# A two-layer graph network whose second neighbour list is gathered in groups of one chunk in place of two

## The reference

```python
x_l = x @ W_l.T + b_l                                    # layer 0
agg = segment_sum(x_l[src], dst)                         # sum over the edges into dst
x = layernorm(x + agg / max(deg, 1)[:, None] + x @ W_r.T)
msg = h[dst] @ W_neigh.T + b_neigh                       # layer 1, h = x
neigh = segment_sum(msg, src)                            # sum over the edges out of src
out = relu(h @ W_self.T + b_self + neigh / max(deg, 1)[:, None])
x = layernorm(x + layernorm(h + out) * gamma + beta)
```

## Time and profile before

| | |
|---|---|
| median of 3 runs | 4260.94 us (4256.3 to 4261.07) |
| span of the profiled execution | 4265.6 us |
| layer 0, placing woven in | 518 to 1850 us |
| layer 0, rest of its chunks | 1850 to 1990 us |
| layer 0, projection | 1990 to 2386 us |
| layer 1, gathering of 928 chunks | 2391 to 3806 us |
| layer 1, projection | 3806 to 4266 us |
| busy in the span: PE, DVE, ACT, POOL | 65%, 61%, 19%, 44% |

### The profile page before, as it was taken

One profiled execution on the slowest core, in us unless ns is written; L12 is line 12 of the kernel. 1 busy time (PEld: TensorE's weight loads), 2 busy tenths in 40 slices (PEclk: granted clock), 3 DMA queues, 4 the chain that ended last, 5 costly groups with the idle time before them and its releaser, 6 DMA issues.

```text
span 4265.6 us, 57125 instructions
## 1 busy us (share of the span) xinstructions
PE 2781.9 (65%) x11308; PEld 1195.8 (28%) x11308; DVE 2610.8 (61%) x6523; ACT 815.1 (19%) x2156; POOL 1897.4 (44%) x2073
## 2 busy tenths in 40 slices
PE   1000188888888888866999655555555555568887
PEld 0000033333333333322455211112111111124443
DVE  3878877777777777754555444444444444448887
ACT  0300044444444444410222000000000000002222
POOL 0600166666666666664000366666666666630000
PEclk9555599999999999977999765665566665669999
DMA  3300066656656666664333566666666666671111
GB/s 140 121 0 0 25 166 166 167 162 165 166 164 164 166 167 166 165 203 136 98 103 103 156 175 178 173 175 173 175 176 176 175 174 170 168 115 59 59 59 49
DMA packets 201222, 586.38 MB, mean 137 GB/s; under 512 B 34672, under 2 KB 35502, under 8 KB 201196
## 3 DMA queue, kind: packets, MB, share of 16 engines
q0 software_dynamic: 148480, 488.56, 42.3%
q1 hardware_dynamic: 52716, 97.53, 7.3%
HBM read 534.51 MB, written 51.44 MB: 137 GB/s over the span
## 4 chain that ended last, share of the span: by engine, by line
PE 39%; DVE 19%; issue 16%; DMA 10%; DVEq 6%; another core or an unknown queue 4%; ACT 2%; SPq 2%; POOL 2%; POOLq 0%; ACTq 0%
PE ps L703 37%; DMA rows<-table,idx_ring 8%; DVE acc L577 4%; DVEq L571 3%; DVE flat L496 2%; DVE onehot L564 2%; POOL rows L359 2%; DVE flat L497 1%; DVE flat L498 1%; DVE where L592 1%; PE ps L805 1%; DVE st L651 1%; PE ps L808 1%; DVE spot L590 1%
## 5 line engine op out<-in xcount | busy, mean ns | idle before, releaser
L359 POOL DMA_INDIRECT rows<-table,idx_ring x1856 | 1794.6, 967 | 1438.0 <-issue 453.5
L703 PE MATMUL ps<-rows,onehot 128*128 128x512 f16 (+1 forms) x5568 | 1378.6, 384 | 782.5 <-DVE acc L577 614.7
L577 DVE TENSOR_TENSOR acc<-acc,ps 128x513 f32 x928 | 638.7, 688 | 850.8 <-remote 328.4
L703 PE MATMUL ps<-where,put 128*128 128x464 f16 x3328 | 801.1, 363 | 380.3 <-ACT put L852 297.8
L703 PEld LDWEIGHTS ps<-rows,onehot 128*128 128x128 bf16 x5568 | 537.3, 113 | 1645.9 <-DVE acc L577 749.2
L564 DVE TENSOR_SCALAR onehot<-iota_node,loc_ring,rows 128x128 bf16<-128x128 f16 x1856 | 583.4, 322 | 281.2 <-DMA rows<-table,idx_ring 250.1
L851 ACT ACTIVATE put<-spot,flat 128x128 f16<-128x128 f16 x832 | 334.1, 402 | 1099.4 <-DVE spot L590 754.3
L703 PEld LDWEIGHTS ps<-where,put 128*128 128x128 f16 x3328 | 267.4, 97 | 696.5 <-issue 371.3
L592 DVE TENSOR_SCALAR where<-iota_chunk,hi_ring 128x928 f16<-128x928 f16 x832 | 380.4, 457 | 0.0
L865 ACT ACTIVATE flat<-acc,rdeg 128x512 f32 (+1 forms) x98 | 69.4, 710 | 1577.5 <-DVE rdeg L640 1574.0
L703 PE MATMUL ps<-w_a,flat 128*128 128x512 f32 x784 | 355.1, 596 | 0.1
(11 more groups left out here) (131 smaller groups left out, 1368.0 us busy)
## 6 DMA issues: line engine op xcount, KB each, us to landing
rows<-table,idx_ring POOLq DMA_INDIRECT x1856
table<-rows SPq DMA_DIRECT2D x98, 257.0 KB, 3.7
h_scratch<-rows SPq DMA_DIRECT2D x49, 256.0 KB, 2.0
rows<-h_scratch SPq DMA_DIRECT2D x49, 256.0 KB, 2.7
acc<-in_x SPq DMA_DIRECT2D x4, 3072.0 KB, 23.5
rows<-in_x SPq DMA_DIRECT2D x48, 256.0 KB, 3.3
out<-rows SPq DMA_DIRECT2D x48, 256.0 KB, 2.0
w_a<-in_w_l_t SPq DMA_DIRECT2D x1, 1024.0 KB
```

What stands on the lines that cost most here:

```text
L359: nc.gpsimd.indirect_dma_start(out=rows[:, k % GB, :], out_offset=None, in_=tables[layer][:, :], in_offset=bass.IndirectOffsetOnAxis(ap=id ...
L577: V.tensor_tensor(tile_acc, tile_acc, part, ALU.add).then_inc(s_acc, 1)
L703: return nc.tensor.matmul(*args, skip_group_check=True, **kw)
```

## The change

The second entry of `GROUP` goes from 2 to 1. `GROUPS[1]` goes from 464 groups of two chunks to 880 of one, so `CHUNKS[1]` goes from 928 to 880; everything else follows from these.

```diff
-    GROUP = (2, 2)
+    GROUP = (2, 1)
     GROUPS = [-(-(-(-E // (P * g)) + T - 1) * g // U) * U // g for g in GROUP]
```

## The result

The changed kernel takes 4395.95 us (median of 4 runs, 4381.14 to 4399.21), the kernel before 4260.99 beside it (4 runs, 4256.3 to 4261.07). The ratio is 1.0311 with a 95% interval of 1.0293 to 1.0328: slower by 3.1%, 135 us. Forecast were 4217 and faster.

A forecast was written before the change was run, and what follows sets the result against it. Between pauses layer 1 was taken as bound by POOL's 1.25 us a chunk, layer 0 with placing by PE and POOL alike. Terms -37 + 9 - 17 + 1 = -44 us took 4260.9 to 4217, range for 8 in 10 4165 to 4275.

The forecast's parts named there:

- a: End of layer 1: 26 empty chunks in place of 48, at 1.67 us each, -37 us.
- b: DVE in layer 1: an add per chunk raises its least time from 0.71 to 1.21 us, just under POOL's 1.25.
- c: Layer 1's real chunks: pauses cost 0.31 a chunk, pace 1.56 us, +9 us; bounds -39 and +95.
- d: PE's waits for adds in layer 1: slot ring of 0.98 us a chunk costs nothing; granted clock at or under 0.62.
- e: Layer 0's placing: 440 columns instead of 464 cut PE's step from 1.24 to 1.20; half of 33 us, -17.
- f: The list: casting 880 elements instead of 464, and the two matmuls ahead of it, +1 us.
- R2: Layer 1: DVE becomes the bound and pays pauses in full, pace 1.66, +42 us, 4303 in all; chance 0.23.
- R1: Layer 1: pauses hold POOL too, so nothing is lost, pace stays 1.503, 4169 us in all; chance 0.24.

The follow-up runs named there:

- r9: The changed kernel, unchanged, run again on a chip without pauses: 3703.87 us against 3781.2 for the kernel before, ratio 0.9793.
- r17: The changed kernel with all three of DVE's loops over chunks written out, layer 0's too; with pauses: 4196.31 us against 4253.57, ratio 0.9864.
- r4: The kernel before, with ACT running eight idle one-column activations for every add of layer 1; with pauses: 4281.29 us against 4252.12, ratio 1.0074.
- r1: The changed kernel without layer 1's register load, all its adds going to tile 0 (sum by tile left out); with pauses: 4186.43 us against 4252.12, ratio 0.9851.
- r3: The changed kernel with four PSUM slots in layer 1 instead of two, adds four groups late; with pauses: 4367.01 us against 4252.12, ratio 1.0276.
- r12: The kernel before with DVE's loop over layer 1's chunks written out, on a chip without pauses: 3780.85 us against 3781.2, ratio 0.9998.
- r8: The kernel before with the placing's matmuls 512 columns wide instead of 464, `where` 48 columns longer; without pauses: 3795.78 us against 3781.03, ratio 1.0036.
- r14: The kernel before with one more unused register load for every chunk of layer 1, on a chip with pauses: 4401.77 us against 4255.14, ratio 1.0346.
- r13: The changed kernel with DVE's loop over layer 1's chunks written out, on a chip with pauses: 4198.23 us against 4255.14, ratio 0.9864.
- r11: The kernel before with one more unused register load for every chunk of layer 1, on a chip without pauses: 3815.86 us against 3781.2, ratio 1.0089.
- r15: r14's kernel with DVE's loop over layer 1's chunks written out, with pauses: 4269.69 us against 4253.57 for the kernel before, ratio 1.0037.
- r18: The kernel before with eight waits on long-reached semaphores ahead of every one-hot of layer 1; no pauses met: 3779.71 us against 3778.91, ratio 1.0003.

## Why the prediction was wrong

The bound itself, POOL at 1.25 between pauses, was read rightly, and so were most steps.

*a, right.* 26 empty gathers in place of 48: forecast -37, measured -38 with pauses; without them 50 us in place of 87.

*b, right in its size.* DVE's adds follow at 1.04 to 1.06 (forecast 1.08) and over a hand-over at 1.77 where no spell falls in (forecast 1.9), so DVE's least time is about 1.05 + (1.77 - 1.05) / 8 = 1.14, under POOL's 1.25. r9, with every gather 1.25 apart, bears it out. The 600 ns of the Trainium skill ("DMA: Bandwidth & Descriptors", Latency and other measured facts) disagree with the traces here: 297 to 334 ns with no spell about (r9), and medians of 302 to 305 with them. The measurement decides.

*c, the step that failed.* It said that "with equal limits on two engines a pause is paid in full, as in layer 0", took a pause as a stop of about 3.6 us every 15 whatever DVE has to do in it, and put the upper bound at 1.66. Measured is 1.748, +170 us in place of +9. On DVE a pause is a spell in which its sequencer goes on in steps of 0.70 us. Of the 9.9 instructions that a chunk now has, some cost such a step each, so that a single chunk fills the spell: 6.99 us from one add to the next in the timeline above, the mean over a hand-over 5.76. That is 4.0 us more than the 1.77 without a spell. Between spells DVE needs 1.05 of the 1.25, so the seven chunks up to the next hand-over make good 7 x 0.20 = 1.4 of the 4.0 at most. DVE never catches up, and POOL, with its eight buffers full, waits: (7 x 1.19 + 5.76) / 8 = 1.76, with 1.19 as the mean step between other adds. The analogy with layer 0 was the fault behind it. There the pace is 1.59 (1.585 to 1.595) with every kernel that was run with pauses, r17's leaner DVE included, so what holds layer 0 isn't what was to be feared in layer 1. The reading that "in these pauses all engines stand" was wrong for DVE: the trace of before had 188 sequencer instructions over 0.6 us in layer 1 to show it. And the thought that more instructions bring more pauses has no support: r4 and r1 have a pause every 12.9 and 12.3 us with 14.3 and 10.8 instructions a us.

*d, in part.* The ring costs nothing without pauses (r9) and some 30 us with them (r3). The granted clock was to be at or under 0.62 and rose to 0.68; no run shows why.

*e, forecast -17, measured +2 with pauses and -10 without* (1087.8 to 1077.8 us, from the first gather to the 833rd, r12 and r9). PE's step fell from 1.24 to 1.20 as forecast. PE had less to do and the stretch with pauses didn't move, so PE isn't its bound there. DVE's sequencer isn't either (r17); DVE's own work, ACT and its sequencer were not tried. What is was not found. Nor is PE's step the pace without pauses, which was 1.31 and is 1.30 (1087.8 and 1077.8 by 832), with PE 96% busy in r12. PE has a share in it there: r8's 48 columns cost 15 us of the whole time.

*f and the rest:* layer 0's first gather came 3 us earlier, not 1 later. Over all the traces it comes at 514 to 518 us, so this is noise, and the 1 us is neither borne out nor refuted.

*The rivals.* With pauses R2 came, in layer 1 and slower as it said, but at 1.748 and +135 in place of 1.66 and +42: DVE with no reserve is the bound. Its price was bounded from above by a stop that doesn't depend on DVE's work. Without pauses the outcome is R1's, that nothing is lost in layer 1, though its reason (pauses that hold POOL as well) has no part there: real chunks -33 (1101 to 1068), the end -37, the placing -10, together -80, of which the spans show -78 (3779.8 and 3701.7).

**What stays open.** What a pause is, and why some chips have none. Each chip was met on one occasion, and what else ran on it isn't known, so the chip can't be told from the occasion. Whether the count of instructions decides alone: r14, r3 and the change have count and reserve against them, and r1 and r13 have both for them. By count, DVE gets through 5.4 to 5.75 instructions a us in these three (9.0 / 1.67, 9.9 / 1.748, 9.9 / 1.714) and at most 5.2 in the others, which looks like a ceiling. For it speaks that r14, whose DVE has less reserve than the change's (its least time is 1.25, and r11's pace without pauses is already 1.287), loses less, and that r15, with nearly the change's reserve, loses next to nothing; r18 was to decide and met no pauses. Which of the instructions take a slow step is open too, and so is why 87 of the changed kernel's 102 spells begin at a hand-over (from 3 us before its first copy to 2 us behind it), where in r13 it is 26 of 78, no more than chance gives. The Trainium skill ("NOTIFIC — the notification-queue block", Overflow: three behaviours, one of which stalls the engine) says that the block that writes the instruction records holds back its producers rather than lose a record inside. No run here shows whether that is what a spell is.

## What to carry to other kernels

Before an instruction is added to an engine's loop, look at the longest duration of its sequencer instructions as well as at the median: a register load at 305 median and 728 longest says that there are times in which it costs more than double, and what an engine loses then grows with how many it has. An engine at 1.14 us beside a bound of 1.25 has a reserve only while nothing stops it; count what it must make good between two pauses, not its step. And where the written-out loop is affordable, it takes away register instructions without touching the work: where there are pauses, the same change went from 3.1% slower to 1.4% faster by it. Last, the same pair of kernels gave +3.1% and -2.1% on different chips, so a result of this size needs the kernel before beside it, and a look at which kind of trace it comes from.

## What was new of the hardware

- The same kernel took 4252 to 4261 us on four occasions (chips 7, 0, 5 and the runs shown) and 3779 to 3781 on three (chips 11, 8, 12), some 12.5% apart, with nothing in between. The whole difference lies in the two gatherings: the projection behind layer 1 takes 459.7 us in the trace of before and 458.7 in that of r12 (the kernel before, written out), and the first gather starts at 518 and 516. The granted clock of the whole is alike (0.815 for the changed kernel with pauses, 0.823 without).
- A slow spell on DVE: steps of 0.70 us for register, branch and wait instructions alike, 3.1 us long in the mean of the kernel before, 5.1 of the changed one, and one every 12.5 to 20 us by kernel, only on the slower chips and (but for single instructions) only where rows are gathered. ACT's sequencer has such steps in layer 0; those of PE and POOL have none in any trace.
- Two waits on reached semaphores are one instruction of 0.05 us on DVE; without pauses, four such instructions a chunk cost nothing (r18).
- TensorE's granted clock in layer 1 rose from 0.62 to 0.68 although PE was busy for less of the stretch, 626 us of 1260 in place of 705.
